# A decoder kernel on one core: in the second layer's attention, six pieces of the round schedule move to later rounds

## What is computed

```
x = x + _L1_attn_ref(_layernorm(x))          # its last product, y @ out_proj_w.T, is the "mix" below
x = x + _L1_xattn_ref(_layernorm(x), ctx, ctx)
    Q = q @ Wq + b_q;  K = ctx @ Wk + b_k;  V = ctx @ Wv + b_v      # 16 heads of 16 channels
    P = softmax(Q @ K.T / sqrt(16));  out = (P @ V) @ Wo + b_o
x = x + _L1_ffn_ref(_layernorm(x))           # its batch norm needs mean and variance of the normed rows
```

## Time and profile before

| | |
|---|---|
| median of 3 runs | 6643.4 us |
| the profiled execution | 6643.99 us |
| its span on the core | 6642.2 us |
| busy: TensorE, its weight loads, VectorE, ScalarE, GpSimd | 89%, 65%, 82%, 53%, 56% |
| this stage | from 4698.1 us (its first matmul) to 5296.7 us (the next stage's first VectorE work) |
| of it the steady part | one sample per 34.77 us |

### The profile page before, as it was taken

How to read it: one execution, slowest core, us unless ns; L and a number is a source line. 1 busy time by engine, 2 the same in 40 slices (tenths; PEclk the granted TensorE clock), 3 DMA queues, 4 the chain that set the end, 5 groups by cost and what they waited for, 6 DMA issues and landing times. The chain is left out here.

```text
span 6642.2 us, 179774 instructions
## 1 busy us (share of the span) xinstructions
PE 5938.0 (89%) x76324; PEld 4289.9 (65%) x76324; DVE 5476.1 (82%) x10790; ACT 3547.0 (53%) x8048; POOL 3729.9 (56%) x1761
## 2 busy tenths in 40 slices
PE   7677776899989899999999999999788789999999
PEld 5566675677767755555555555555566578888888
DVE  7899996555558799999999999999666588888886
ACT  6455553333324487878888888888355422222221
POOL 1587883111101199999999999999322122222222
PEclk9788888999999999999999999999899999999999
DMA  3332211011003321121211112120121100000000
GB/s 101 82 88 68 56 49 60 30 58 43 28 23 142 126 55 40 52 47 38 59 39 53 43 41 50 35 62 15 56 88 57 46 7 8 8 8 8 8 8 7
DMA packets 390880, 314.63 MB, mean 47 GB/s; under 512 B 171702, under 2 KB 358841, under 8 KB 389564
## 3 DMA queue, kind: packets, MB, share of 16 engines
q1 hardware_dynamic: 384390, 302.84, 15.8%
q10 hardware_dynamic: 5686, 0.29, 0.1%
HBM read 194.99 MB, written 108.01 MB: 46 GB/s over the span
## 5 line engine op out<-in xcount | busy, mean ns | idle before, releaser
L2397 POOL TENSOR_TENSOR ss_ch<-ss_h,ss_c_all 128x2048 f32<-128x2048 f32 x511 | 2325.5, 4631 | 33.7 <-DVE ss_h L2426 23.2
L2426 DVE TENSOR_TENSOR_SCAN ss_h<-ss_decay,banks 128x1024 f32<-128x1024 f32 x1024 | 2256.5, 2266 | 63.9 <-PE banks L2313 63.3
L2313 PE MATMUL banks<-ss_diag,ss_dxT 128*32 128x256 f32 x32768 | 1970.2, 381 | 25.9 <-DVE ss_h L2426 17.2
L2313 PEld LDWEIGHTS banks<-ss_diag,ss_dxT 128*32 128x32 f32 x32768 | 1008.0, 110 | 808.2 <-DVE ss_h L2426 196.1
L2377 ACT ACTIVATE ss_decay<-ss_dt,ss_neg_a 128x510 f32<-128x510 f32 x2048 | 1358.3, 711 | 257.1 <-DVE ss_h L2426 250.9
L2765 POOL TENSOR_TENSOR pk_blockhot<-pk_onehot,pk_parts 128x2048 bf16<-128x2048 bf16 x96 | 345.4, 3627 | 923.0 <-DVE pk_parts L2991 923.0
L2368 ACT ACTIVATE ss_diag<-ident,ss_bT 128x128 f32<-128x128 f32 x2016 | 685.5, 387 | 184.4 <-PE banks L2313 184.4
L2320 PE MATMUL banks<-ss_ch,ss_stacked 128*32 128x256 f32 x8192 | 635.6, 382 | 44.9 <-POOL ss_ch L2397 40.0
L812 PE MATMUL banks<-ms_rprod,ident 128*128 128x128 f32 x2048 | 463.9, 398 | 224.3 <-POOL ms_rprod L937 221.6
L812 PEld LDWEIGHTS banks<-ms_rprod,ident 128*128 128x128 f32 x2048 | 430.6, 257 | 251.5 <-POOL ms_rprod L937 191.8
L1051 POOL TENSOR_SCALAR l_ln_mv<-l_ln_mv 128x2 f32<-128x2 f32 x64 | 14.9, 233 | 985.2 <-DVE l_ln_mv L1046 985.2
(11 more groups left out here) (330 smaller groups left out, 9910.8 us busy)
## 6 DMA issues: line engine op xcount, KB each, us to landing
ss_dt<-keep_dt SPq DMA_DIRECT2D x256, 128.0 KB, 4.1
ss_c_all<-keep_cn SPq DMA_DIRECT2D x512, 64.0 KB, 2.1
keep_v<-ms_cx_values SPq DMA_DIRECT2D x32, 512.0 KB, 2.8
l_va<-keep_v SPq DMA_DIRECT2D x32, 512.0 KB, 4.5
l_kf<-keep_k SPq DMA_DIRECT2D x32, 256.0 KB, 2.9
keep_x<-l_x SPq DMA_DIRECT2D x32, 256.0 KB, 2.1
keep_xc<-si_xc SPq DMA_DIRECT2D x16, 512.0 KB, 4.1
keep_zs<-si_zs SPq DMA_DIRECT2D x16, 512.0 KB, 5.1
```

The source lines that it names most:

```text
L2313: m = T_.matmul(inp[u % 2][s * CB:(s + 1) * CB, g, :, t * P:(t + 1) * P], inputs[i % 2][0][:, g, t, u * CB:(u + 1) * CB], diag[slot][:, g, ...
L2397: G_.tensor_tensor(ch[u // 2 % 4][:, :, :, :, :].rearrange("p j g n t -> p j (g n t)"), h[u // 2 % 4][:, :, :, :, :].rearrange("p j g n t ...
L2426: V.tensor_tensor_scan(whole(h[u // 2 % 4][:, u % 2, :, :, :]), whole(decay[u % 4]), whole(inp[u % 2]), 0.0, ALU.mult, ALU.add).then_inc(s ...
```

## The change

- The divided attention is turned in round 5 (22) and projected in round 6 (23), one round later; VectorE adds the result in round 6, the bias in round 7, takes the statistics in round 8 and norms in round 10.
- The normed rows of that sample are turned two rounds later, in round 12 (29), the batch statistics come in round 13 (30).
- The entering sample's normed rows are turned in round 3 and the query is projected in round 5, one round later each. VectorE norms them in round 1 as before.
- The query's parts are cut one round later (rounds 8 to 12, repeated in 13), ScalarE's repeated copies in round 14.
- VectorE adds the mix two rounds later, in round 14.

```diff
-    VALUES, PROJECTED = (5, 9, 13, 17), 22
+    VALUES, TURN_BACK, PROJECTED, NORMED = (5, 9, 13, 17), 19, 23, 29
...
-            if r == self.PROJECTED - 3:
+            if r == self.TURN_BACK:
                 turn_back()
             if r == self.PROJECTED - 1:
                 T_.wait_ge(*self.divided.at(b))
                 turn(T_, bank[self.AFTER0], self.att, self.chip.ident, self.att_turned.sem)
             if r == self.PROJECTED:
                 project_out()
-            if r == self.PROJECTED + 5:
+            if r == self.NORMED:
                 T_.wait_ge(*self.norm2.normed.at(b))
...
         m.then_inc(self.divided.sem, 1)
-        yield
-        yield
+        yield from nothing(3)
         V.wait_ge(*self.projected.at(b))
...
-                + [(enter_tensor(T_, b), b, at.ENTERS + 4) for b in range(B)]
+                + [(enter_tensor(T_, b), b, at.ENTERS + 5) for b in range(B)]
...
-                + [(at.finish_vector(V, b, x_ready), b, at.PROJECTED - 3) for b in range(B)]
+                + [(at.finish_vector(V, b, x_ready), b, at.TURN_BACK) for b in range(B)]
                 + [(enter_vector(V, b), b, at.ENTERS) for b in range(B)]
-                + [(at.parts_vector(V, b), b, at.ENTERS + 9) for b in range(B)]
-                + [(measure(V, b), b, at.PROJECTED + 6) for b in range(B)]
-                + [(mix_vector(V, b), b, at.MIX + 4) for b in range(B)])
+                + [(at.parts_vector(V, b), b, at.ENTERS + 10) for b in range(B)]
+                + [(measure(V, b), b, at.NORMED + 1) for b in range(B)]
+                + [(mix_vector(V, b), b, at.MIX + 6) for b in range(B)])
...
-                + [(at.enter_scalar(A, b), b, at.ENTERS + 4) for b in range(B)]
-                + [(at.parts_scalar(A, b), b, at.ENTERS + 15) for b in range(B)])
+                + [(at.enter_scalar(A, b), b, at.ENTERS + 5) for b in range(B)]
+                + [(at.parts_scalar(A, b), b, at.ENTERS + 16) for b in range(B)])
```

More of the change, by code:

```diff
@@ L1561, in project_out @@
             m.then_inc(self.projected.sem, 1)
-        for r in range(self.PROJECTED + 6):
+        for r in range(self.NORMED + 1):
             if r == 0:
```

## The result

| | before | changed |
|---|---|---|
| median | 6641.8 us (8 runs, 6636.2 to 6645.4) | 6620.7 us (8 runs, 6618.7 to 6623.7) |
| ratio | | 0.9970, 95% interval 0.9962 to 0.9979 |
| profiled execution, span | 6644.0, 6642.2 | 6619.8, 6618.0 |
| stage, first mix matmul to the next stage's first VectorE work | 598.6 | 577.9 |
| steady period | 34.77 | 33.33 |

The change makes the kernel 0.30% faster, 21.1 us by the medians. The forecast was 16.9 us and 6626.5. The stage alone became 20.7 us shorter, so the gain is where the change is.

The account below looks back on a forecast made before the run. TensorE's 4.4 us of standstill per period was taken as the bound; 0.93 + 0.45 - 0.34 = 1.04 us per period over 13 periods plus the ends gave 16.9 us, so 6626.5 us (own range 6621 to 6631, all cases 6617 to 6635).

Parts of the forecast that it names:

- What bounds the kernel, and the sign: No engine is full; TensorE is nearest, losing 4.4 us per 34.77 us period, and a gain must come from that.
- 1.14 + 0.38 - 0.37 - 0.22 = 0.93 us per period gained: Rounds 2 to 6: division wait and s(5)-s(6) alternation go; new waits before s(3), round 3's score start, and q heads come.
- the alternation: Where both engines do little, each score waits for the reduce before it: 1.27 us from one score's start to the next.
- the round-2 reduce starts only at 4959.27, behind the 1.10 us of norming: Reason given for round 3's score coming at 4960.10 instead of 4959.73, 0.37 us of new wait on TensorE.
- Rounds 6 to 9: nothing.: VectorE keeps three extras behind the round-6 reduce, so the 1.05 us wait of round 8's score stays.
- 0.45 us gained: Rounds 9 to 12, later turn of the normed rows: 6.35 us become 5.90, from 0.29 of wait and 0.16 of gaps.
- s(15) is 0.34 us late: Round 15's score start: copy and batch statistics behind round 13's reduce delay the next reduce to 1.60 us instead of 1.26.
- ScalarE's copies at 0: Moving ScalarE's 1.46 us of copies to round 14 costs nothing if one raise slips ahead of them; otherwise 1.46.
- The third rival: ScalarE's copies delay both raises and round 0's values by up to 1.46 us: 2.1 us slower, 6645.5 us; chance 0.06.
- More is gained: Rival: reduces run ahead, so new waits and the 0.34 vanish; 1.97 us a period, 6614 us; chance 0.13.
- The waits come back as waits for the reduce: Rival: VectorE sets the pace through the one score bank, about a third of the gain is left, 6638 us; chance 0.15.
- The ends of the stage: Outside the steady periods: sample 12's empty rounds add 0.5 us, sample 13 gives 2.3, sample 14 and first rounds 0.6 together.

Follow-up runs that it names:

- y1: Changed kernel with the divided attention turned and copied in round 4 again, its projection still in 6: median 6633.2 us, period 34.21 us.
- x3: Changed kernel with the normed rows turned in round 11 instead of 12, batch statistics in 12: median 6629.4 us, period 34.08 us.
- x4: Changed kernel with the batch statistics taken 9 rounds later, in round 5: median 6615.8 us, period 33.00 us.
- x1: Kernel before with only the divided attention's turn, projection and what follows one round later: 6635.6 us, ratio 0.9991 to before, period 34.18 us.
- y2: Changed kernel with the mix's addition in round 12 again: one execution, 6624.1 us, period 33.33 us.
- y3: Changed kernel with the batch statistics in round 5 and the query's bias in round 7 instead of 6: median 6618.7 us, period 33.19 us.
- x2: Changed kernel with the entering rows turned in round 2 and the query projected in round 4 again: median 6619.8 us, period 33.23 us.

## Why the prediction was right

- **What bounds the kernel, and the sign.** Right. The gain came out of TensorE's standstill, and undoing either turn puts its wait and its price back (y1, x3).
- **"1.14 + 0.38 - 0.37 - 0.22 = 0.93 us per period gained".** Measured 1.28. Both new waits came as computed, and so did the cover for the alternation between s(5) and s(6). The mis-sized step is "TensorE waits 1.14 us for it, and these 1.14 us go": I took the bracket as the loss. By starts, the q heads at 4960.61 and the turn at 4962.15 in the earlier trace rows stand 1.54 apart where the heads take 0.22, so 1.32 were lost. The turn itself took 0.49 after the stop (4962.15 to 4962.64) and takes 0.44 without one (4956.37 to 4956.81), 0.05 more. And the entering turn, which the earlier trace rows show without a bracket, stood 0.35 behind its k heads in round 2 (4959.07 to 4959.42), where a turn that waits for nothing stands 0.23 behind k heads (the attention's now): a hidden wait of 0.12 for the norming that ended at 4959.27. 1.32 + 0.05 + 0.12 = 1.49 in place of 1.14, and 0.93 + 0.35 = 1.28.
- **"the round-2 reduce starts only at 4959.27, behind the 1.10 us of norming".** The 0.37 us are right, and the reason given for them is not. The reduce starts 0.42 us behind its score (4958.85 to 4959.27), as it does where VectorE stood idle before it (4982.71 to 4983.13), and 0.42 behind it in the changed kernel too (4953.05 to 4953.47). So it waited for its score, and the norming only happened to end then. s(2) to s(3) takes 1.25 because that is the alternation, as from s(6) to s(7) (1.26 in both kernels): the 0.37 is the price of leaving round 2 with nothing special on TensorE. No run moved the norming, but by these rows moving it would give nothing here.
- **"Rounds 6 to 9: nothing."** Right: 6.54 us in both.
- **"0.45 us gained" in rounds 9 to 12.** Measured 0.51; I had priced the turn at 0.50 from a row behind a wait, and it takes 0.44 without one (4974.25 to 4974.69).
- **"s(15) is 0.34 us late".** Measured 0.33, and x4 gives exactly that back. By the sentence of the Trainium skill that the prediction cites (VectorE: DVE Perf Modes, section The DRAIN you can't avoid) the three would take 1.85 us; they take 1.60. The same section goes on to say that a next op which is not held starts earlier, and these rows agree with that.
- **ScalarE's copies at 0.** Right. One raise slipped in front and the last one ends where it did, s(16) stands 1.26 behind s(15) in the changed kernel as before, and x4 moves s(15) without touching them. The third rival, slower through ScalarE, did not happen.
- **The two other rivals.** "More is gained" (6614) had the right suspicion, that the terms were small, but for another reason than its own: the new waits it doubted are all there. "The waits come back as waits for the reduce" is what the earlier trace rows seem to show by their sums, 31.0 us grown to 41.5, but the brackets of a period tell what they are: 0.33 more before s(15) and 0.22 before s(3), which are the terms of 0.34 and 0.37 in the sum, and 0.22 before s(16), which costs nothing (1.26 behind s(15) as before). That makes 0.77 a period, 10.0 us over 13 periods, and the 26 places by which 58 became 84. x1, x3 and y1 each moved the period by nearly what their own place says.
- **The ends of the stage.** Twelve full periods gave 12 x 1.44 = 17.2 us where the forecast has 12.5. The period with sample 12's attention gave 2.1 (forecast 1.5), that with sample 13's 2.0 (2.3), the first rounds 1.1, and the very end lost 1.7, where I had 0.6 for both. Sum 20.7 against 16.9. The loss at the end is not the schedule's, as the last section shows: y2, with the same instructions there, gained 0.5 at it.

So the mechanism and its places were right, and one reason was wrong at no cost. The size was off: 1.44 us a period where the sum has 1.04, almost all of it in one term. That the whole stage was off by only a fifth is partly luck, since the clock took 2.2 us back at its end.

## What to carry to other kernels

Where matmuls are pipelined, price a wait by the distance from start to start, less what the instruction between takes anywhere it runs freely, and not by the idle time in the bracket: here the bracket told 1.14 of the 1.37 us that the stop cost, and another wait, of 0.12, had no bracket at all. In a schedule of rounds with two engines in alternation, as this one, a producer needs a full round between itself and its reader, and each round has only as much room on the second engine as the alternation leaves (here 0.56 us beside each reduce, and up to 3.7 where TensorE has both projections). Before moving an instruction into such a room, list everyone who waits for it, banks included: y3 lost more than it gained to a reader that its sum had left out.

## What was not expected of the hardware

The changed kernel and y2 differ in nothing that runs behind the last sample's maxima, yet from the cast of those maxima to the end of the stage one took 35.7 us and the other 33.5. The granted clock of TensorE tells them apart. The windows of the changed kernel from the last sample's turn back on, with the columns of the earlier trace rows (PEclk, behind the five engines, is the granted clock):

```profile
5262.00:5264.00 2.00, 1.09 (x8) 0.86 (x8) 0.63 (x3) 0.41 (x1) 0.00 (x0) 1.00 0.00 0
5264.00:5266.00 2.00, 1.09 (x4) 0.69 (x4) 0.64 (x2) 0.18 (x1) 0.00 (x0) 0.69 0.00 0
5266.00:5271.00 5.00, 3.78 (x8) 2.50 (x8) 0.69 (x2) 0.40 (x1) 0.00 (x0) 0.50 0.00 0
5271.00:5276.00 5.00, 1.12 (x4) 0.72 (x4) 2.42 (x7) 0.10 (x1) 0.92 (x2) 0.50 0.07 23
```

The same stretches of y2:

```profile
5263.70:5265.70 2.00, 1.09 (x8) 0.86 (x8) 0.44 (x2) 0.59 (x1) 0.00 (x0) 1.00 0.00 0
5265.70:5267.70 2.00, 0.66 (x4) 0.42 (x4) 0.83 (x3) 0.38 (x1) 0.00 (x0) 1.00 0.00 0
5267.70:5272.70 5.00, 1.99 (x8) 1.44 (x8) 2.38 (x6) 0.20 (x1) 0.14 (x1) 1.00 0.00 0
5272.70:5277.70 5.00, 1.12 (x4) 0.71 (x4) 1.49 (x4) 0.59 (x1) 0.79 (x2) 0.50 0.15 52
```

Behind the same turn back, with the same wait of 1.14 us for the division, the clock went to half (1.2 of 2.4 GHz) just as the attention's turn began in one execution (a mean of 0.69 over 5264 to 5266 puts the fall at about 5264.8, and the turn starts at 5264.69), and only before the normed rows' turn in the other. The eight matmuls of the last projection took 3.78 us in the one and 1.99 in the other, the four of the turn before 1.09 and 0.66. In x2 the clock fell as early (35.7 us from cast to end), in x1 within the projection, whose eight matmuls took 3.28 (34.9 to the end); in all other runs, and before the change, that stretch took 33.0 to 34.0 us. Whether the changed kernel does so in every execution stays open, since each kernel has one profile. It costs or spares 2.2 us, the size of this stage's smaller terms, so the end of a stage in which TensorE runs dry is no place to read a schedule's gain from.
